# Token lengths added by TensorE products of 40 rows, and the first load's distances put between two halves of the last load's statistics

## What is computed

```
xn   = layernorm(x)
Dist = sqrt(max(|a|^2 + |xn|^2 - 2 a.xn, 0))     64 context tokens by 512 tokens
R    = dynamic time warping cost of Dist; path = its way back
x    = x + (sum over the path of the context tokens aligned with each token)
x    = x + ffn(layernorm(x))                       8-bit quantised, 256 -> 1024 -> 256
```

## Time and profile before

| | us |
|---|---|
| median of 3 runs | 178.14 (177.49 to 178.94) |
| profiled execution | 177.57 |
| its span | 175.8 |
| DVE busy | 152.1 (87%) |
| PE busy | 113.3 (64%) |
| ACT busy | 107.6 (61%) |
| POOL busy | 38.8 (22%) |

### The profile page before, as it was taken

One profiled execution on the slowest core, in us unless ns is written; L12 is line 12 of the kernel. 1 busy time (PEld: TensorE's weight loads), 2 busy tenths in 40 slices (PEclk: granted clock), 3 DMA queues, 4 the chain that ended last, 5 costly groups with the idle time before them and its releaser, 6 DMA issues.

```text
span 175.8 us, 3392 instructions
## 1 busy us (share of the span) xinstructions
PE 113.3 (64%) x1065; PEld 78.3 (45%) x1065; DVE 152.1 (87%) x724; ACT 107.6 (61%) x203; POOL 38.8 (22%) x102
## 2 busy tenths in 40 slices
PE   6999880000045894000009779999999999999991
PEld 6898760000033681000003326665666666666680
DVE  4899999999999999999999389998899989896361
ACT  3698467899997010135050189877777786878720
POOL 7777764000000000000000000023041323222250
PEclk9999996555555559755555999999999999999998
DMA  5997008400019930020212421006373738192848
GB/s 143 355 348 234 6 4 326 184 0 0 2 52 334 347 107 0 0 76 0 75 62 85 63 37 22 4 0 63 56 72 53 64 61 89 31 105 28 109 48 191
DMA packets 19553, 16.86 MB, mean 96 GB/s; under 512 B 5712, under 2 KB 19152, under 8 KB 19408
## 3 DMA queue, kind: packets, MB, share of 16 engines
q1 hardware_dynamic: 14288, 12.69, 22.7%
q0 software_dynamic: 3808, 3.67, 17.8%
q10 hardware_dynamic: 1440, 0.30, 0.8%
HBM read 7.48 MB, written 9.18 MB: 95 GB/s over the span
## 4 chain that ended last, share of the span: by engine, by line
DVE 45%; PE 35%; DMA 7%; SPq 4%; issue 3%; ACT 3%; ACTq 0%; DVEq 0%
PE y L1389 14%; PE h L1370 9%; DVE Y L1151 6%; DVE R L925 6%; DMA X<-in_x_dram 5%; PE t L1370 5%; SPq L356 4%; DVE A L897 3%; DVE enter L1134 3%; DVE carry L915 3%; DVE bcarry L1133 3%; DVE M L916 3%; PE e L1329 3%; DVE Y L1148 2%; DVE Dm L886 2%
## 5 line engine op out<-in xcount | busy, mean ns | idle before, releaser
L531 POOL DMA_DIRECT2D out_dram<-E x14 | 17.0, 1217 | 125.6 <-DVE E L1120 125.6
L1389 PE MATMUL y<-w2T,XT 128*128 128x256 bf16 x240 | 35.8, 273 | 0.0
L1389 PEld LDWEIGHTS y<-w2T,XT 128*128 128x128 bf16 x240 | 23.3, 98 | 14.0 <-DVE XT L1064 0.3
L719 ACT ACTIVATE h_int<-h,b_s 128x512 int16<-128x512 f32 x37 | 25.3, 686 | 4.9 <-PE h L1370 4.3
L1410 PE MATMUL h<-w1T 128*128 128x512 bf16 x21 | 6.9, 487 | 24.8 <-DVE enter L1134 24.8
L1370 PE MATMUL h<-M,w1T 128*128 128x512 bf16 x74 | 21.9, 380 | 0.8 <-ACT M L712 0.7
L1309 PE MATMUL t<-ident_bf,w_raw 128*128 128x128 bf16 x32 | 4.6, 312 | 25.5 <-ACT w_raw L653 23.9
L1110 DVE TENSOR_SCALAR XT<-h_int 128x1024 bf16<-128x1024 int16 x28 | 12.1, 439 | 8.2 <-ACT h_int L719 8.2
L1410 PEld LDWEIGHTS h<-w1T 128*128 128x128 bf16 x21 | 2.3, 120 | 29.0 <-DVE enter L1134 25.6
L719 ACT ACTIVATE h_int<-t,b_s 128x512 int16<-128x512 f32 x19 | 13.0, 686 | 3.4 <-PE t L1370 3.2
L1309 PEld LDWEIGHTS t<-ident_bf,w_raw 128*128 128x128 bf16 x32 | 3.1, 148 | 27.1 <-issue 24.1
(11 more groups left out here) (236 smaller groups left out, 298.9 us busy)
## 6 DMA issues: line engine op xcount, KB each, us to landing
X<-in_x_dram SPq DMA_DIRECT2D x8, 512.0 KB, 8.4
out_dram<-E POOLq DMA_DIRECT2D x14, 256.0 KB, 4.5
w_raw<-in_L_ffn_w_dram SPq DMA_DIRECT2D x2, 1024.0 KB, 5.8
out_dram<-b_s SPq DMA_DIRECT2D x2, 1024.0 KB, 5.9
out_dram<-b_s SPq DMA_DIRECT2D x2, 768.0 KB, 9.4
S<-in_ctx_dram SPq DMA_DIRECT2D x1, 512.0 KB, 4.3
out_dram<-E SPq DMA_DIRECT2D x4, 128.0 KB, 3.2
path_dram<-A SPq DMA_DIRECT2D x3, 160.0 KB, 1.8
```

The costliest lines, as they stand in the source:

```text
L531: nc.gpsimd.dma_start(tiles_out[:, b:b + 2, quad_of(g, 2 * h), :], res[:, g % 2, 2 * h:2 * h + 2, :], accum_op=ALU.add).then_inc(out_store ...
L719: nc.scalar.activation(h_int[:, g % 2, n, :], hidden_banks[i % 3][:, :], ACT.Identity, bias=b1_s[:, n:n + 1], scale=1.0 / W_ONE).then_inc( ...
L1389: mm = nc.tensor.matmul(results(g, t, t + 1)[:, 0, :], hq[:, g % 2, n, t * P:t * P + P], w2T[:, n, :], start=(n == 0 and not bias), stop=( ...
```

## The change

- The length is added before the scaling, in PSUM, by products of 40 rows: rows 0 to 7 hold s of the tokens of one tile each, with weights D(1 + mean^2 + var) of the context; rows 32 to 39 hold r with weight -D eps. Divided by s later, it is the same length.
- To have s as rows, `spread_rows` gets a product that transposes the sums of squares (128 columns beside the 16), ACT takes the root of 144 columns instead of 16, and DVE the reciprocal of rows 32 to 39 (`inverse_rows`) besides that of the lanes (`inverse_lanes`).
- The scaling takes the clamp with it; `lengthened`, `token_lengths`, `token_gap`, the clamps of ACT and of `last_distances` and the array `lengths` go.
- The context lengths come as 8 rows (`len_of`, 8 columns for each q) in place of 32 equal rows per column group, and ACT copies them into the weights. POOL makes the constant parts: three memsets more and two affine selections.
- DVE's order: reciprocal rows 0, half of the statistics of load 3, load 0, the other half, and the rest as below. PE's order: length products of a load follow later work, the turns of load 3 are parted, and the products of load 3 come in three calls by column groups and halves. ACT takes the roots of load 0 before the turns of load 3; copies of load 1 are parted by the first deviation.

```diff
# DVE
-            scales(0)
-            load_moments(3)
-            scales(1)
+            inverse_rows(0)
+            for j in range(B // 2):
+                moments(LOADS - 1, j)
+            inverse_lanes(0)
             turned(0)
             scaled(0)
-            lengthened(0)
-            scales(2)
+            inverse_rows(1)
+            for j in range(B // 2, B):
+                moments(LOADS - 1, j)
+            inverse_rows(2)
+            inverse_lanes(1)
             turned(1)
             scaled(1)
-            lengthened(1)
+            inverse_lanes(2)
             order_numbers()
+            inverse_rows(3)
+            order_masks()
             turned(2)
-            scales(3)
+            inverse_lanes(3)
             scaled(2)
-            lengthened(2)
             last_distances(0)
             last_distances(1)
-            order_masks()
...
+            def inverse_rows(k):
+                v.wait_ge(std_ready, k + 1)
+                rows = deviations[GAP_AT:ROWS, k, SW:SW + P]
+                nc.vector.reciprocal(rows, rows).then_inc(rows_ready, 1)
...
+                nc.vector.scalar_tensor_tensor(out=flat(norms[:, k, :, :, :]), in0=flat(turned_back[:, k % 2, :, :, :]), scalar=0.0,
+                                               in1=scale_by(k), op0=ALU.max, op1=ALU.mult).then_inc(prods_made, 1)
# PE
+            def dots(k, hs=(0, 1), qs=range(NQ)):
+                pe.wait_ge(xT_copied, (UL // 2) * k + max(qs) + 1)
...
+            def add_lengths(k, hs=(0, 1)):
+                pe.wait_ge(rows_ready, k + 1)
+                for h in hs:
+                    flat = dist_banks[k if k < LOADS - 1 or h == 0 else 0][:, :, :].rearrange("p a b -> p (a b)")
+                    for e in range(2):
+                        at = P * (2 * e + h)
+                        rows = deviations[0:ROWS, k, SW:SW + P] if e == 0 else deviations[0:ROWS, k, SW + P - 1:SW - 1:-1]
+                        mm = nc.tensor.matmul(flat[:, at:at + P], row_weights[:, e, h, :], rows, start=False,
+                                              stop=(e == 1 and h == hs[-1]))
                 mm.then_inc(dot_done, 1)
...
+                nc.tensor.matmul(spread_bank(k)[:, SW:SW + P], row_sums[:, k, :], ident[:, :], start=True,
+                                 stop=True).then_inc(spread_done, 1)
...
                 for q in range(NQ):
+                    mm = nc.tensor.matmul(bank23[0][0:B, :, :].rearrange("p a b -> p (a b)")[:, P * q:P * q + P],
+                                          len_of[:, B * q:B * q + B], ident[:, :], start=True, stop=True)
...
-            dots(0)
+            dots(0).then_inc(dots_taken, 1)
             pe.wait_ge(std_ready, 1)
             spread_rows(1)
             turns(2)
-            dots(1)
+            add_lengths(0)
+            dots(1).then_inc(dots_taken, 1)
             pe.wait_ge(std_ready, 2)
             spread_rows(2)
-            turns(3)
+            turns(3, 0, 2)
+            add_lengths(1)
             dots(2)
             spread_rows(3)
-            pe.wait_ge(std_ready, 3)
-            dots(3)
+            add_lengths(2)
+            turns(3, 2, 4)
+            pe.wait_ge(std_ready, LOADS)
+            dots(3, (0, 1), (0, 1))
+            dots(3, (0,), (2, 3))
+            add_lengths(3, (0,))
+            dots(3, (1,), (2, 3))
+            add_lengths(3, (1,))
# ACT
+            copy_xT(1, 0)
+            copy_xT(1, 1)
             spread(0)
+            copy_xT(1, 2)
+            copy_xT(1, 3)
             spread(1)
             for j in range(UL // 2):
                 copy_xT(2, j)
-                if j % 2:
-                    token_gap(j // 2)
+            roots(0)
             spread(2)
-            for j in range(UL // 2):
-                copy_xT(3, j)
-                if j == 1:
-                    token_gap(2)
-            roots(0)
+            copy_xT(3, 0)
+            copy_xT(3, 1)
             spread(3)
-            token_gap(3)
+            copy_xT(3, 2)
+            copy_xT(3, 3)
             roots(1)
             roots(2)
-            for hs in range(2):
-                roots(LOADS - 1, hs)
+            last_roots(0)
+            last_roots(1)
# POOL
+            nc.gpsimd.memset(len_of[:, :], 0.0).then_inc(rows_const, 1)
+            nc.gpsimd.memset(row_sums[:, :, :], 0.0).then_inc(rows_const, 1)
+            nc.gpsimd.memset(row_weights[:, :, :, :], 0.0).then_inc(rows_const, 1)
+            pool.wait_ge(rows_const, 3)
+            for e in range(2):
+                weights = row_weights[:, e, :, :].rearrange("p h (q i) -> p h q i", q=NQ)
+                nc.gpsimd.affine_select(out=weights, in_=weights, compare_op=ALU.not_equal, fill=-D * EPS, base=-GAP_AT,
+                                        pattern=[[-1, 2], [-2, NQ], [0, TW]], channel_multiplier=1).then_inc(rows_const, 1)
...
-            token_lengths(0)
-            token_lengths(1)
             spread_of(LOADS - 1)
-            token_lengths(2)
-            token_lengths(LOADS - 1)
```

More of the change, by code:

```diff
@@ L34 @@
 UL = 2 * CL
+SW = 2 * UL
+GAP_AT = TW
+ROWS = GAP_AT + B
 NG = NU // 4
@@ L481, in spread_of @@
                     pool.wait_ge(lanes_made, 3)
-                nc.gpsimd.tensor_tensor(spread_parts[:, k, :, :], centred_sum[:, us].unsqueeze(2).to_broadcast([P, B, NQ]),
+                nc.gpsimd.tensor_tensor(spread_parts[:, k, :, :], row_sums[:, k, 0:B].unsqueeze(2).to_broadcast([P, B, NQ]),
                                         quarter[:, :].unsqueeze(1).to_broadcast([P, B, NQ]), ALU.mult).then_inc(parts_ready, 1)
[L485 to L496, removed]
             pool.wait_ge(ctx_split, 1)
-            pool.wait_ge(ctx_len_ready, 1)
+            pool.wait_ge(ctx_len_ready, 2)
             nc.gpsimd.tensor_tensor(S_r1[:, :, :], S[:, :, :], S_hi[:, :, :], ALU.subtract).then_inc(ctx_rest, 1)
@@ L535, in _, with roots, last_roots @@
         def _(act):
[L536 to L542, removed]
+            def roots(k):
+                act.wait_ge(prods_made, 2 * (k + 1))
                 act.wait_ge(pool_const, 4)
                 for e in range(2):
-                    if hs is None:
-                        act.wait_ge(clamped, k + 1)
                     n0 = CL * k if e == 0 else NC - CL - CL * k
[L548 to L553, removed]
+                    dst = bass.AP(E, 2 * CH * e + n0 * (TW + 1), [[SLOTS * EW, P], [CH, 2], [TW + 1, CL], [EW, HR]])
+                    nc.scalar.activation(dst, norms[:, k, e, :, :].rearrange("p (h c) i -> p h c i", h=2),
+                                         ACT.Sqrt).then_inc(rooted, 1)
+            def last_roots(hs):
+                k = LOADS - 1
+                act.wait_ge(prods_made, 2 * k + 2 * (hs + 1))
+                across = 2 * CH + (NC - CL - 2 * CL * k) * (TW + 1)
+                dst = bass.AP(E, CH * hs + CL * k * (TW + 1), [[SLOTS * EW, P], [across, 2], [TW + 1, CL], [EW, HR]])
+                part = half_of_load(norms[:, k, :, :, :], hs).rearrange("p (e c) i -> p e c i", e=2)
+                nc.scalar.activation(dst, part, ACT.Sqrt).then_inc(rooted, 1)
             def spread(k):
@@ L826, in _ @@
             link(nc.vector.tensor_tensor(ctx_len[:, :], ctx_mv[:, :, 0], ctx_mv[:, :, 0], ALU.mult))
-            nc.vector.tensor_tensor(ctx_len[:, :], ctx_len[:, :], ctx_mv[:, :, 1], ALU.add).then_inc(ctx_len_ready, 1)
+            v.wait_ge(rows_const, 1)
+            for h in range(2):
+                lanes = slice(I * h, I * h + I)
+                nc.vector.scalar_tensor_tensor(out=len_of[lanes, h:h + (B + 2) * (NQ - 1) + 1:B + 2], in0=ctx_len[lanes, :],
+                                               scalar=1.0, in1=ctx_mv[lanes, :, 1], op0=ALU.add,
+                                               op1=ALU.add).then_inc(ctx_len_ready, 1)
             def scale_by(k):
-                return rstd[:, k, :, :].rearrange("p e u -> p (e u)").unsqueeze(2).to_broadcast([P, 2 * UL, HR])
+                return rstd[:, k, :, :].rearrange("p e u -> p (e u)").unsqueeze(2).to_broadcast([P, SW, HR])
             def flat(t):
@@ L1237, in dots @@
                         for kk in range(KH):
-                            for q in range(NQ):
+                            for q in qs:
                                 tokens = XT[:, k % 2, 2 * q + h, kk, :] if e == 0 else XT[:, k % 2, 2 * q + h, kk, P - 1::-1]
                                 mm = nc.tensor.matmul(flat[TW * q:TW * q + TW, at:at + P], ST[:, q, kk, h, HR * e:HR * e + HR],
-                                                      tokens, start=(kk == 0), stop=(kk == KH - 1))
+                                                      tokens, start=(at == first and kk == 0), stop=False)
+                return mm
+            def add_lengths(k, hs=(0, 1)):
+                pe.wait_ge(rows_ready, k + 1)
+                for h in hs:
+                    flat = dist_banks[k if k < LOADS - 1 or h == 0 else 0][:, :, :].rearrange("p a b -> p (a b)")
+                    for e in range(2):
```

(4 more changed lines are left out.)

112 lines of the change are left out of this document (46 added, 66 removed).

## The result

| | before | after |
|---|---|---|
| median of 4 runs, us | 178.13 (177.49 to 178.94) | 180.25 (179.91 to 180.35) |
| ratio | | 1.0113, 95% interval 1.007 to 1.0157 |
| profiled execution, its span | 177.57, 175.8 | 180.35, 178.6 |
| first transposition of E | 31.49 | 33.53 |
| from there to the start of the last scaling | 140.52 | 140.49 |

The forecast was 179.8, 0.9% slower; it came at 180.25, 1.1% slower. The page's slices of PE and DVE, against the earlier trace rows: PE is now full from the third slice to the seventh, and DVE has holes in the seventh and eighth (6 and 6), where it was full.

A forecast was written before the change was run, and what follows sets the result against it. DVE and PE were both taken as full; after the change PE ends last, moving E's first transposition from 31.49 to 33.2 us. That +1.7 us on the median 178.14 gave 179.8, range 178.0 to 181.8.

The forecast's parts named there:

- DVE's added reciprocals: Four DVE reciprocals over 8 partitions x 128, 0.75 us each with gap, 3.0 us in all; lower bound 0.35 each.
- the weights' delay: Weight loads issued from 31.6 instead of 25.68 us; 1.4 us later for ACT, absorbed in the 6.4 us before NL_more.
- four waits for PE: DVE idles for PE's results before turning loads 0 and 1 and before each half of the last load.
- sums of load 0 start: PE begins load 0's sums at 12.75 us: 12.11 before, plus 0.6 for context lengths in one 8-column place.
- stop marked "issue": PE's 0.72 us pause before 18.54 in load 1's products, unexplained by any semaphore, was expected to stay.
- three length calls of a load: PE's length products for loads 0 to 2, full passes of 109 ns with changes of shape, about 0.85 us each.
- three quarters of the last products: PE's first two calls of load 3's products, run partly side by side, from 27.4 to 29.25 us.
- Rival 2: PE's pause in load 1's products does not return: PE 0.72 us earlier, end 0.7 us earlier, 179.1 us; chance 0.14.
- The second call of the last load: PE's products of column groups 2 and 3, first half, can run beside those of groups 0 and 1.
- rival 1: Column groups keep strict program order, so the last load's second call follows the first: 0.87 us more, 180.7; chance 0.28.
- The work taken from DVE: Three length additions, and two additions and two clamps in the last load: 4.1 us busy, taken as 3.6.
- The 0.6 us added: The profiled execution, 177.57 us, lay 0.6 us under the median 178.14; the shift was added to that median.

The follow-up runs named there:

- the kernel without lengths: Changed kernel with length products cut to one product of 8 columns per call, other lengths left out: 177.36 us, 0.9941 of before.
- the kernel with 128 rows: Changed kernel with length products over 128 rows, zero weights in the added ones, instead of 40: 179.82 us, 1.0083 of before.
- the kernel with halves: Changed kernel with the last load's products in two calls by halves over all four column groups, not three calls by pairs: 180.25 us, 1.0136 of before.
- the fourth of before: Fourth profiled execution of the unchanged kernel: 178.56 us, first transposition of E at 32.41.
- the kernel with turns first: Changed kernel with last load's products in two calls by halves and its last two turns before load 2's length products: 179.01 us, 1.0039 of before.
- third execution of before: Third profiled execution of the unchanged kernel: 178.95 us, first transposition of E at 32.72.
- the one pass: Changed kernel with sums of squares and context lengths turned in one pass instead of two: 179.50 us, 1.0062 of before.
- lighter PE kernel: Changed kernel with halves, turns first, 128 rows, one-pass sums and context lengths, and POOL's context subtraction after load 2's parts: 177.31 us, 0.9942 of before.

## Why the prediction was right, and where it wasn't

**What bounds.** Right: PE ends last, DVE's added reciprocals cost nothing, the weights' delay is absorbed, and from PE's last result to E it took 1.64 us (forecast 1.65). Of the four waits for PE that the forecast gave DVE (0.65, 0.2, 0.25 and 0.65 us), three came (0.40, 1.34 and 0.73); the one before load 1's transposition did not.

**PE's steps.** Its last result released DVE at 31.89 us, forecast 31.55. The 0.34 us are what is left of terms that nearly cancel:

| step of PE | forecast | measured | difference |
|---|---|---|---|
| sums of load 0 start | 12.75 | 12.21 | -0.54 |
| stop marked "issue" | 0.7 | none | -0.70 |
| three length calls of a load | 0.85 each | 1.09, 1.08, 1.08 | +0.70 |
| length call between the last products | 0.55 | 0.64 | +0.09 |
| three quarters of the last products | 1.85 | 2.34 | +0.49 |
| all else | | | +0.30 |

- The stop was kept "since they came after so many instructions and not after a semaphore". It did come after so many, as the kernel without lengths shows; but PE now reaches that record at 18.97 us, later than the 18.54 at which it went on before. By the forecast's own steps, with these products from 18.3, it would have come there near 19.0: the stop was kept without asking when PE gets to it. Rival 2's event, then, though rival 2 put the stop down to the load of x.
- Of the length products the pass was right (109 ns, whatever the rows) and the changes too small: the added 0.1 us each way is the change between 40 and 128 rows, as the kernel with 128 rows showed.
- The second call of the last load was to run beside the first. It began 1.34 us after it, at 28.51, though ACT's copies were there at 27.92 (26.84 + 1.08), and only some 0.4 us of the two overlap. In the kernel with halves the first product follows the same copies by 0.15 us (28.06). So rival 1 was half true: a column group can pass another, as in the earlier trace rows, but here only by a few products. The Trainium skill ("TensorE: Matmul & The Clock Gate", Part 3, "The mechanism") has matmuls start and end in program order. Here the starts don't: `y` of the later call starts at 28.51, before `e` of the earlier one at 28.83.
- The sums of load 0 came early because PE did. Its first eight turned tiles took 1.02 us (6.32 to 7.34) and in the profile before 1.52 (6.56 to 8.08, the row below), whose pace the forecast kept. This differs between executions: the fourth of before has 1.02 too, the kernel with turns first 1.50. The granted clock reads 1.00, the level of 2.4 GHz, in both stretches; what sets the pace is not shown. Having come early, PE waited 0.18 us for POOL, whose parts were there at 12.06, near the forecast's 12.2. In the kernels with turns first and with 128 rows PE came at 12.5 and did not wait.

```profile
6.56 1.59 PE L1271 MATMUL h<-ident,X 128*128 128x128 f32 x8
```

**DVE's steps.** The reciprocal of 128 elements takes 943 ns, forecast 724; the order numbers took 0.46 us (0.20 + 0.26), forecast 1.25. Neither matters here: with shorter reciprocals E moved by 0.01 us. The work taken from DVE was put at 3.6 us; by the starts of its rows before it is 3.8.

**From the span to the time.** Here the reasoning failed and the sum came out all the same, by luck. The 0.6 us added, because the profiled execution lay under the median, were x's late landing. After the change nothing waits for x there (the second half of the statistics starts at 20.84 with no wait), so they had no place: against the third execution of before, E is only 0.81 us later (33.53 - 32.72). In their place came a longer end, 4.14 us against 3.3 to 3.4, which the forecast took to be unchanged. The two spans are 1.5 us apart: 0.8 at the front, 0.7 behind it.

## What to carry to other kernels

When an edit moves work between two full engines, step through the receiving one call by call, with its changes of shape, and see whether its last result still comes ahead of the other's; once it doesn't, the other engine's savings are worth nothing. Look at the receiving engine's order first (here the turns ahead of the length products gave 0.90 us, the 128 rows 0.55 and the one pass 0.48), and let a product keep the shape of its neighbours even if rows go unused. Before building on one profiled execution, see where its time lies among the runs: a gap to the median may be a wait that the edit hides. And where an engine stops behind a certain record, ask when the changed kernel gets to that record.

## What the runs showed of the hardware

- RECIPROCAL on DVE takes 237 ns for 16 elements and 943 for 128, 6.3 ns for each further one, where 4 and 16 in the earlier trace rows gave 4.4. The groups by line and shape after:

```profile
L868 DVE RECIPROCAL deviations<-deviations 8x128 f32<-8x128 f32 x4 | 3.8, 943 | 0.4 <-ACT deviations L559 0.3
...
L877 DVE RECIPROCAL rstd<-deviations 128x16 f32<-128x16 f32 x4 | 0.9, 237 | 0.0
```

- Some of DVE's instructions are longer beside POOL's. The order numbers took 0.67 and 0.56 us before, while POOL subtracted lengths, and 0.20 and 0.26 after, with POOL idle. The rows of DVE and POOL before:

```profile
22.98 0.69 DVE L848 TENSOR_TENSOR h_int<-h_int,lengths 128x512 f32<-128x512 f32 x1
23.59 0.67 DVE L796 TENSOR_SCALAR order_low<-order_raw 128x192 int32<-128x192 int32 x1
24.29 0.56 DVE L797 TENSOR_SCALAR order<-order_low 128x192 f32<-128x192 int32 x1
...
23.00 1.73 POOL L492 TENSOR_TENSOR lengths<-aa,length_gap 128x256 f32<-128x256 f32 x2
```

Not all are: the addition that started 0.02 us before POOL's kept its 0.69 us, and the two others of its kind, begun while POOL was at work, took 0.99. In the lighter PE kernel a scaling of 0.69 us took 1.24, with POOL's subtraction beside it, while the transposition just before it, beside the same subtraction, kept its 0.72:

```profile
16.99 2.14 POOL L522 TENSOR_TENSOR h_int<-S,S_hi 128x1024 f32<-128x1024 f32 x1
```
